# Router products and the norm statistics made as the tiles of the second graph layer finish, and one scale and shift for both norms

## The chip, the cores and the metric

The kernel runs on one NeuronCore of one Trainium2 chip. The metric is the device time of one execution in microseconds. Five engines run side by side and meet only through semaphores: TensorE (PE) for matrix products, VectorE (DVE), ScalarE (ACT), GpSimd (POOL), which here computes the addresses of gathers and scatters, and SyncE (SP), which only starts transfers and relays semaphores.

## The reference

N = 6250 nodes with D = 256 channels, 106250 edges in the first graph layer. Four layers follow each other, each added to its own input:

```python
x = x + gnn0(layernorm(x), ...)          # attention over edges
x = x + slice_ffn(layernorm(x)[None], ...)[0]
x = x + gnn1(layernorm(x), ...)          # attention over the same edges
x = x + experts(layernorm(x)[None], ...)[0]

def experts(x):                          # cut to what matters
    logits = x @ Wr + br                 # Wr is 256 x 8
    top_p, top_idx = top 2 of softmax(logits)
    weights = top_p / top_p.sum(-1)
    xn = (x - mean(x)) * rsqrt(var(x) + 1e-5)       # the second norm
    xe = xn[None] * ln_g[:, None] + ln_b[:, None]
    h = gelu(einsum('end,edh->enh', xe, W1) + b1);  y = einsum('enh,ehd->end', h, W2) + b2
    return (weights * y of the two chosen experts).sum(1)
```

The experts layer is given `layernorm(x)`, so the router sees a normed row, and the experts see a row that has been normed twice.

## The kernel before, in words

The nodes lie on 128 partitions in QT = 49 tiles of 128 rows (`K["x"]`, 128 x 49 x 256 in SBUF, node order sorted by degree). The program runs in stages: `sort_nodes`, `graph` layer 0, `slice_ffn`, `graph` layer 1, `experts`. A stage is a block in which each engine has its own instruction stream, and a barrier ends it.

**`graph` (L713), both layers.** Each tile of nodes has a run of chunks; a chunk holds C = 4 edges for each of the 128 nodes. There are 232 chunks in a layer, about 4.7 for each tile. How many a tile has is a number read at run time, so `by_tile` (L768 and on) is a loop over tiles around a loop over chunks, with the first ("opens") and last ("closes") chunk of a tile written out apart. For each chunk: SP loads the records (L791) and relays to the others that rows have landed (L796); POOL issues four gathers of 128 rows (L826) into a ring of R = 4 chunk buffers, and takes a buffer again only when DVE has made that chunk's messages (`msg_ok`); DVE makes the attention scores (L1017, L1020, L1022, L1023), ACT the exponentials (L915 to L920), DVE rescales the running sums (L987) and makes the messages (L980), and PE sums them in PSUM (L864, L866). When DVE has made the messages of a tile's first chunk it runs `finish` for the tile before (L989 to L999): the denominator, its reciprocal, the division into `fin`, and the addition to `K["x"]`. The next chunk's L1017 stands right behind `finish` on DVE. Layer 0 has another `finish` (without L999), and its DVE does more for each chunk: L967 on 128x1024 and a reduction L1013 over 128x1088 instead of L1017 and L987.

**`experts` (L1552), first block: the router.** On SP: loads of `wr`, `br`, eight of 1 MB of W2 (L1631), small ones, then the stores of the rows `xall` to HBM (`tok`, L1640, seven groups). On POOL: a few iotas, then 49 scatters of `K["x"]` into the output (L1832). DVE makes the statistics of the first norm with BN_STATS in a loop of seven tiles an iteration (`Norm.statistics`, L130 to L135), and their variance (L141 to L147); ACT takes the square root (L1690); DVE the reciprocal and the bias (L152, L153). Then a loop over tiles runs on three engines: ACT norms the tile twice (L1696 into `xrow`, L1697 into `xall`), PE transposes it (L1653), ACT copies the transpose out of PSUM (L1705), PE multiplies it with `wr` (L1662), DVE adds `br` (L1740) and takes the statistics of the normed tile for the second norm (L128). Only then can DVE choose the two best experts of each row (L1751 to L1759), ACT scale and shift `xall` once more (L1721), and DVE and PE build the lists of rows of each expert: ranks from a product with a triangle (L1675), positions (L1774 to L1796), and 98 pairs of one-hot tiles (L1802, L1803) which PE multiplies (L1684). L1818 is DVE's last instruction of the block. The second block runs the experts; PE bounds it.

`Chain.link` (L60) makes an instruction count up a semaphore and the next one wait for it.

## Time and profile before

| | |
|---|---|
| median of 3 runs | 5204.4 us (5200.88 to 5206.28) |
| span of the profiled execution, first to last instruction | 5182.1 us |
| median of the runs less that span | 22.3 us |
| busy: PE / DVE / POOL / ACT | 3347.4 / 2375.1 / 2286.8 / 1277.0 us |

The profile gives no time of the profiled execution other than its span; what lies around the span is taken to be the 22.3 us. Stages by the trace: graph layer 0 from about 504 to 2146 us, slice_ffn to 2609, graph layer 1 to 4176, router block to 4375, experts to the end. "Busy" leaves out register, branch and semaphore instructions; the trace lists those of DVE as "DVEq". "idle before" is the time in which an engine ran nothing before an instruction, with what ended it; "issue" means that the profile shows nothing that it waited for.

### The profile page before, as it was taken

Reading aid. Unit: us, or ns where it says so; the run is one execution under the profiler, and the core shown is the slowest. Engines: PE = TensorE matmul, PEld = TensorE weight load, DVE = VectorE, ACT = ScalarE, POOL = GpSimd, SP = SyncE. Lnnn points to the kernel's source line nnn. Section 1 sums busy time; section 2 is a strip of 40 time slices with the busy share of each in tenths; the row PEclk is TensorE's granted clock in tenths of the full one; section 3 lists DMA queues with packets and bytes.
Section 4 is the critical chain, followed back from the end, with each engine's and each line's share of the span. In section 5 each row is a group of like instructions: output and inputs, shape, how many; then the busy total and the mean of one; then the engine's idle time right before and its main releaser. Section 6 shows DMA issues by size and latency. Waiting matters only on the chain. (4 is left out here: it accounts for less than half of the span.)

```text
span 5182.1 us, 77256 instructions
## 1 busy us (share of the span) xinstructions
PE 3347.4 (65%) x13712; PEld 2377.0 (46%) x13713; DVE 2375.1 (46%) x5239; ACT 1277.0 (25%) x5289; POOL 2286.8 (44%) x2343
## 2 busy tenths in 40 slices
PE   4500676767777777598935545554555537999998
PEld 3300343444444444365823333333333335889887
DVE  4500566656666666776434444444444436111111
ACT  2200333333333333242300000000000034333333
POOL 5160555555555555200355555555555540333333
PEclk9855888888888888798967777777777757999999
DMA  8441333333333333200133333333333342666665
GB/s 200 127 127 32 81 81 76 82 76 81 84 83 81 81 79 83 49 0 1 47 78 86 82 84 85 85 86 84 84 85 85 85 124 96 172 171 171 172 171 136
DMA packets 298776, 489.07 MB, mean 94 GB/s; under 512 B 151906, under 2 KB 199984, under 8 KB 298216
## 3 DMA queue, kind: packets, MB, share of 16 engines
q0 software_dynamic: 127312, 325.41, 25.7%
q1 hardware_dynamic: 158637, 158.21, 10.4%
q10 hardware_dynamic: 12770, 4.81, 0.4%
q8 instruction: 21, 0.34, 0.0%
q14 instruction: 36, 0.29, 0.0%
HBM read 430.09 MB, written 58.63 MB: 94 GB/s over the span
## 5 line engine op out<-in xcount | busy, mean ns | idle before, releaser
L826 POOL DMA_INDIRECT g_rows<-rows,g_recs x1856 | 1759.0, 948 | 1562.6 <-DVE g_msg L980 832.2
L864 PE MATMUL g_pA<-g_msg,k_ident 128*128 128x264 f32 x3712 | 1102.1, 448 | 150.8 <-DVE g_msg L980 91.1
L864 PEld LDWEIGHTS g_pA<-g_msg,k_ident 128*128 128x128 f32 x3712 | 795.0, 225 | 501.3 <-issue 360.7
L855 PE MATMUL g_pE<-g_ew,g_recT 128*128 128x512 f32 x936 | 597.0, 772 | 419.3 <-ACT g_recT L895 373.7
L866 PE MATMUL g_pA<-g_accs,k_ident 128*128 128x264 f32 x928 | 353.6, 467 | 663.4 <-DVE g_accs L987 517.0
L980 DVE TENSOR_TENSOR g_msg<-g_rows,g_pp 128x1024 f32 (+1 forms) x464 | 564.9, 1218 | 417.4 <-ACT g_pp L920 332.3
L915 ACT ACTIVATE g_msg<-g_dd (+1 forms) x464 | 113.5, 245 | 1827.8 <-DVE g_dd L1023 1228.3
L866 PEld LDWEIGHTS g_pA<-g_accs,k_ident 128*128 128x128 f32 x928 | 185.6, 220 | 766.2 <-DVE g_accs L987 570.8
L855 PEld LDWEIGHTS g_pE<-g_ew,g_recT 128*128 128x128 f32 x936 | 202.7, 233 | 648.4 <-issue 584.6
L1969 PE MATMUL e_pY<-e_w,e_hT 128*128 x1632 | 375.1, 383 | 22.6 <-issue 21.9
L1958 PEld LDWEIGHTS e_pH<-e_xT,e_w 128*128 128x128 f32 x3264 | 382.3, 193 | 5.2
L1958 PE MATMUL e_pH<-e_xT,e_w 128*128 128x128 f32 x3264 | 382.7, 276 | 0.0
L1916 POOL DMA_INDIRECT out<-e_ys,e_goal x102 | 160.7, 1576 | 493.8 <-issue 468.7
L1969 PEld LDWEIGHTS e_pY<-e_w,e_hT 128*128 128x128 f32 x1632 | 301.9, 190 | 72.6 <-issue 34.8
L1013 DVE TENSOR_REDUCE g_al<-g_prod (+1 forms) x232 | 296.9, 1280 | 72.0 <-issue 69.6
L967 DVE SCALAR_TENSOR_TENSOR g_prod<-g_pE,g_dall (+2 forms) x232 | 284.2, 1225 | 89.1 <-issue 68.2
L2054 DVE TENSOR_TENSOR e_ys<-e_pY,k_x 128x256 f32<-128x256 f32 x102 | 43.3, 424 | 577.1 <-PE e_pY L1969 577.1
L938 ACT ACTIVATE g_accs<-g_pA,g_cs 128x33 f32 x1464 | 285.9, 305 | 59.9 <-issue 36.2
L2011 ACT ACTIVATE e_hT<-e_pH,e_b 128x128 f32<-128x128 f32 x816 | 222.2, 383 | 44.7 <-issue 42.0
L987 DVE TENSOR_TENSOR g_accs<-g_pA,g_cs 128x264 f32 x232 | 146.6, 632 | 161.3 <-issue 132.1
L1998 ACT ACTIVATE e_xT<-e_pX,e_bl,e_gl 128x128 f32<-128x128 f32 x204 | 82.4, 454 | 470.8 <-PE e_pX L1941 470.8
L1017 DVE TENSOR_TENSOR g_al<-g_rows,k_sdst (+2 forms) x232 | 44.3, 191 | 331.5 <-issue 302.3
(410 smaller groups left out, 3575.4 us busy)
## 6 DMA issues: line engine op xcount, KB each, us to landing
e_w<-in_L_ffn_W SPq DMA_DIRECT2D x110, 1024.0 KB
g_rows<-rows,g_recs POOLq DMA_INDIRECT x1856
g_recs<-slots SPq DMA_DIRECT2D x468, 8.0 KB
tok<-e_xall SPq DMA_DIRECT2D x7, 910.0 KB
rows<-p_row SPq DMA_DIRECT2D x50, 119.0 KB
own<-p_row SPq DMA_DIRECT2D x50, 119.0 KB
p_x<-in_x SPq DMA_DIRECT2D x1, 5600.0 KB
own<-p_x SPq DMA_DIRECT2D x1, 5600.0 KB
```

Source lines behind the costliest of these rows:

```text
L826: pool.indirect_dma_start(out=rows[:, r, j, :], out_offset=None, in_=rows_d, in_offset=bass.IndirectOffsetOnAxis(ap=recs[:, r, 4 * j:4 * j ...
L855: last = t_.matmul(pE[:, b, c:c + 512], recT[:, b, :], ew[:].rearrange("p c d -> p (c d)")[:, c:c + 512], start=True, stop=True)
L864: t_.matmul(pA[:, b, 0:MW], K["ident"][:], msg[:, b, j, :], start=(j == 0), stop=False)
L866: t_.matmul(pA[:, b, 0:MW], K["ident"][:], accs[:], start=False, stop=True).then_inc(agg_ok, 1)
L938: last = s.activation(to[:, h, :], of[:, h, :], ACT.Copy, scale=cs[:, 0, h:h + 1])
L967: v.scalar_tensor_tensor(to, row_of(pE[:, b2, :]).rearrange("p (c h w) -> p c h w", c=C, h=H), 0.0, over(by_head(row_of(dall[:, bass.ds(t, ...
L980: v.tensor_tensor(to, of, by, ALU.mult).then_inc(msg_ok, 1)
L1013: ch.link(v.reduce_sum(sc, prod[:, b2, :, :].rearrange("p a g w -> p (a g) w"), axis=AX), wait=False)
L1916: pool.indirect_dma_start(out=out, out_offset=bass.IndirectOffsetOnAxis(ap=goal_b[b][:, 0:1], axis=0), in_=ys[:, b, :], in_offset=None, bo ...
L1958: last = t_.matmul(pH[b][c][:, j, :], w1[:, b, k, units], xT[:, b, k, :], start=(k == 0), stop=(k == 1))
L1969: last = t_.matmul(pY[b][:], hT[:, b, k, :], w2[:, bass.ds(e, 1), k, :].rearrange("p a h -> p (a h)"), start=(k == 0), stop=(k == KC - 1))
L2011: last = s.activation(hT[:, b, c * HK + j, :], pH[b][c][:, j, :], ACT.Gelu, bias=b1[:, bass.ds(e, 1), c * HK + j])
```

## The change

It acts on graph layer 1 and on the router block.

In graph layer 1, `finish` no longer ends with the addition of the tile to `K["x"]`. Behind it DVE takes BN_STATS of the tile (for the first norm), multiplies the unnormed tile with all eight columns of Wr at once (128 x 8 x 256 products; Wr lies transposed and copied to all partitions) and sums over the 256 channels, into `raw`, 8 numbers for each row. Wr's copy is a transfer of 128 x 2048 floats, 1 MB, at the head of SP's stream, and DVE sums it over channels once (`wsum`) before the first chunk.

The router block has no loop any more. With r = 1/std, the logits are raw * r + nbias * wsum + br. The second norm's variance follows from the first one's: the normed row has mean 0 and variance a * r * r, so `std2` is sqrt(a * r * r + eps), and both norms together are one scale and one shift. ACT norms `xall` straight from `K["x"]`, once: seven tiles before the exponential, 42 behind it.

```diff
@@ graph, layer 1
+            norm, wsum, raw = K["norm"], K["wsum"], K["raw"]
+            wr = m.sb(L + "wr", [Q, X, D])
+            by_expert = m.sb(L + "by_expert", [Q, X, D])
@@ block.sync
                 n2 = groups(sp, K)
+                if not first_layer:
+                    sp.dma_start(wr[:].rearrange("p e k -> p (e k)"), ins["L1_ffn_Wr"]...broadcast_to([Q, X * D])).then_inc(wr_in, 16)
@@ block.vector
                 dve.wait_ge(w_zero, 3)
+                if not first_layer:
+                    dve.wait_ge(wr_in, 16)
+                    v.reduce_sum(wsum[:], wr[:], axis=AX)
@@ finish
-                    fc = Chain(dve, fch, (2 if first_layer else 3) * t)
+                    fc = Chain(dve, fch, (2 if first_layer else 6) * t)
...
-                        v.tensor_tensor(to, to, fin[:], ALU.add).then_inc(x_ok, 1)
+                        fc.link(v.tensor_tensor(to, to, fin[:], ALU.add))
+                        norm.tile(v, t, xk[:, bass.ds(t, 1), :])
+                        fc.link(v.tensor_tensor(by_expert[:], over(to, 1, X), wr[:], ALU.mult))
+                        fc.link(v.reduce_sum(row_of(raw[:, bass.ds(t, 1), :]), by_expert[:], axis=AX), wait=False)
@@ experts, block.sync
-                    sp.dma_start(wr[:], ins["L1_ffn_Wr"]...).then_inc(w_in, 16)
@@ experts, block.tensor: turn, product and their loop go
@@ experts, block.scalar
-                    normed (L1696, L1697), turned (L1705) and their loop
                     act.wait_ge(stats2, 1)
-                    s.activation(norm2.rstd[:], norm2.rstd[:], ACT.Sqrt).then_inc(sq2, 1)
+                    s.activation(std2[:], std2[:], ACT.Sqrt).then_inc(sq2, 1)
+                    act.wait_ge(rst2, 1)
+                    def normed(t):
+                        s.activation(xall[:, t, 0:D], x3[:, t, :], ACT.Identity, bias=norm.nbias[:, t:t + 1],
+                                     scale=norm.rstd[:, t:t + 1]).then_inc(row_ok, 1)
+                    for t in range(GT):
+                        normed(t)
                     act.wait_ge(e_in, 1)
                     s.activation(best[1][:], best[1][:], ACT.Exp).then_inc(e_out, 1)
+                    for t in range(GT, QT):
+                        normed(t)
@@ experts, block.vector
-                    norm1.statistics(dve, v, x3)
...
-                    logits (L1736 to L1740) and its loop, norm2.variance
+                    ch.link(v.tensor_tensor(std2[:], norm.a[:], norm.rstd[:], ALU.mult))
+                    ch.link(v.tensor_tensor(std2[:], std2[:], norm.rstd[:], ALU.mult))
+                    v.tensor_scalar(std2[:], std2[:], LN_EPS, None, ALU.add).then_inc(stats2, 1)
+                    dve.wait_ge(rst1, 1)
+                    v.tensor_tensor(tmp[:], over(norm.nbias[:], 2, X), over(wsum[:], 1, QT), ALU.mult)
+                    ch.link(v.tensor_tensor(lg[:], raw[:], over(norm.rstd[:], 2, X), ALU.mult))
+                    dve.wait_ge(w_in, 16)
+                    v.tensor_tensor(tmp[:], tmp[:], over(br[:], 1, QT), ALU.add)
+                    dve.wait_ge(sq2, 1)
+                    ch.link(v.reciprocal(std2[:], std2[:]))
+                    ch.link(v.tensor_tensor(lg[:], lg[:], tmp[:], ALU.add))
+                    v.tensor_tensor(norm.rstd[:], norm.rstd[:], std2[:], ALU.mult)
+                    v.tensor_tensor(norm.nbias[:], norm.nbias[:], std2[:], ALU.mult).then_inc(rst2, 1)
...
-                    norm2.scales(v, ch, rst2)
```

## Rows read from the trace of the kernel before

**Rows 1.** Busy time by stretch: stretch, length, PE, PEld, DVE, ACT, POOL busy, clock, DMA share, GB/s.

```profile
518.50:2142.00 1623.50, 1154.16 (x3465) 670.75 (x3465) 1010.82 (x1530) 572.33 (x2890) 868.35 (x917) 0.86 0.32 80
2622.00:4170.30 1548.30, 804.10 (x2310) 530.91 (x2310) 660.21 (x1579) 99.64 (x693) 872.58 (x921) 0.74 0.34 84
4175.70:4305.40 129.70, 62.66 (x294) 57.13 (x294) 50.19 (x165) 63.45 (x149) 48.90 (x56) 0.51 0.38 115
4305.40:4375.50 70.10, 46.78 (x204) 32.63 (x204) 65.82 (x258) 25.97 (x52) 0.00 (x0) 0.79 0.27 94
```

**Rows 2.** Waits of POOL, 2622 to 4170 us: waiter, releaser, us in total, times, longest.

```profile
POOL g_rows L826 <- DVE g_msg L980: 388.8, 104, 8.7
```

**Rows 3.** Waits of DVE in the same stretch.

```profile
DVE g_al L1017 <- issue: 302.3, 122, 12.0
```

**Rows 4.** Line L826, 2622 to 4176 us: durations in ns (min/median/max), first and last start.

```profile
L826 POOL DMA_INDIRECT g_rows<-rows,g_recs x921: 941/947/1086, 2621.3 to 4154.4; - x185
```

**Rows 5.** Timeline of DVE around one finish: start, length, what, idle before.

```profile
2889.84 1.22 DVE L980 TENSOR_TENSOR g_msg<-g_rows,g_pp 128x1024 f32 x1 [0.26 <-issue]
2891.14 0.17 DVE L991 TENSOR_SCALAR g_den<-g_pA 128x8 f32 x1
...
2892.26 0.42 DVE L999 TENSOR_TENSOR k_x<-k_x,g_fin 128x256 f32 x1
2892.88 0.19 DVE L1017 TENSOR_TENSOR g_al<-g_rows,k_sdst  x1 [0.20 <-issue]
...
2895.18 1.22 DVE L980 TENSOR_TENSOR g_msg<-g_rows,g_pp 128x1024 f32 x1 [0.24 <-ACT g_pp L920]
```

**Rows 6.** Timeline of POOL over the same finish.

```profile
2891.85 0.95 POOL L826 DMA_INDIRECT g_rows<-rows,g_recs  x1 [4.59 <-DVE g_msg L980]
...
2897.19 0.95 POOL L826 DMA_INDIRECT g_rows<-rows,g_recs  x1 [0.64 <-issue]
```

**Rows 7.** Groups of DVE instructions over the span: count, busy, mean ns of one.

```profile
L1013 DVE TENSOR_REDUCE g_al<-g_prod x231 | 295.7, 1280 | 69.6 <-issue 69.6
L1281 DVE TENSOR_TENSOR f_lg<-f_lg,f_top 128x512 f32<-128x512 f32 x49 | 33.9, 692 | 1.7
L1280 DVE TENSOR_REDUCE f_top<-f_lg 128x8 f32<-128x512 f32 x49 | 33.6, 686 | 1.7
L128 DVE BATCH_NORM_STATS2 e0b_st<-e_xall x48 | 20.5, 427 | 15.8 <-issue 13.7
```

**Rows 8.** Timeline of DVE in the router block.

```profile
4176.86 12.19 DVE L128 BATCH_NORM_STATS2 e0a_st<-k_x  x37 [1.24 <-PEq L106]
...
4212.50 0.10 DVE L1729 MEMSET e0a_na<- 128x49 f32 x1 [2.42 <-issue]
...
4214.69 0.47 DVE L152 RECIPROCAL e0a_rstd<-e0a_rstd 128x49 f32<-128x49 f32 x1 [0.31 <-issue]
...
4305.44 0.56 DVE L1751 TENSOR_REDUCE e_best<-e_lg 128x49 f32<-128x392 f32 x1
4306.03 0.57 DVE L1752 TENSOR_TENSOR e_tmp<-e_lg,e_best 128x392 f32<-128x392 f32 x1
...
4374.18 0.22 DVE L1818 TENSOR_SCALAR e_first_of<-e_second 128x106 f32<-128x106 f32 x1
```

**Rows 9.** Line L133, the statistics loop's branch, 4176 to 4187 us: ns min/median/max.

```profile
L133 DVEq COMPARE_BRANCH  x4: 56/61/69, 4178.3 to 4184.1; - x4
```

**Rows 10.** The same branch, 4190 to 4216 us.

```profile
L133 DVEq COMPARE_BRANCH  x2: 696/1042/1389, 4196.3 to 4214.5; - x2
```

**Rows 11.** Line L1832, POOL's scatters of the router block.

```profile
L1832 POOL DMA_INDIRECT out<-k_x,k_pt x49: 957/963/1556, 4177.9 to 4238.7; - x49
```

**Rows 12.** Timeline of SP in the router block.

```profile
4317.01 20.95 SPq L1640 DMA_DIRECT2D tok<-e_xall  x7
```

**Rows 13.** Timeline at the head of graph layer 1.

```profile
2609.42 2.41 SPq L791 DMA_DIRECT2D g_recs<-slots  x4
...
2612.48 0.99 POOL L826 DMA_INDIRECT g_rows<-rows,g_recs  x1 [13.94 <-DMA g_recs<-slots]
```

**Rows 14.** The chain that ended last: start, length, what.

```profile
4375.50 5.19 DMA k_x<-in_L_ffn_b
```

More of the change, by code:

```diff
@@ L1615, in experts @@
             pL = m2.ps("e0_pL", [Q, 512])
-            pT = [m2.ps(f"e0_pT{b}", [128, 2, 128]) for b in range(2)]
-            pG = [m2.ps(f"e0_pG{b}", [Q, X]) for b in range(2)]
             pR = m2.ps("e0_pR", [Q, 512])
@@ L1627, in _ @@
                 def _(sp):
-                    sp.dma_start(wr[:], ins["L1_ffn_Wr"].rearrange("(k p) e -> p k e", p=128)).then_inc(w_in, 16)
                     sp.dma_start(br[:], ins["L1_ffn_br"].unsqueeze(0).broadcast_to([Q, X])).then_inc(w_in, 16)
@@ L1700, in turned @@
-                    def turned(t, b, early):
-                        act.wait_ge(t_ok, t + 1)
-                        if not early:
-                            act.sem_inc(pace, 1)
-                            act.wait_ge(g_ok, t - 1)
-                        s.activation(xtT[:, b, :, :], pT[b][:, :, 0:Q], ACT.Copy).then_inc(xtT_ok, 1)
-                    def group(u, first, last_group):
-                        for b in range(3 if last_group else 2):
-                            if b < 2 or not last_group:
-                                normed(2 * u + (b + 1), (b + 1) % 2)
-                            turned(2 * u + b, b % 2, first)
@@ L1716, in _ @@
+                    for t in range(GT):
+                        normed(t)
                     act.wait_ge(e_in, 1)
                     s.activation(best[1][:], best[1][:], ACT.Exp).then_inc(e_out, 1)
-                    act.wait_ge(rst2, 1)
-                    for t in range(QT):
-                        s.activation(xall[:, t, 0:D], xall[:, t, 0:D], ACT.Identity, bias=norm2.nbias[:, t:t + 1],
-                                     scale=norm2.rstd[:, t:t + 1]).then_inc(row_ok, 1)
+                    for t in range(GT, QT):
+                        normed(t)
@@ L1727, in _ @@
                     ch = Chain(dve, vch)
-                    norm1.statistics(dve, v, x3)
-                    ch.link(v.memset(norm1.a[:], 0.0))
-                    norm1.variance(v, ch, stats1)
+                    ch.link(v.memset(norm.a[:], 0.0))
+                    norm.variance(v, ch, stats1)
                     dve.wait_ge(sq1, 1)
-                    norm1.scales(v, ch, rst1)
-                    dve.wait_ge(w_in, 32)
-                    def logits(t, b):
-                        dve.wait_ge(xt_ok, t + 1)
-                        norm2.tile(v, t, xt[:, bass.ds(t, 1), :])
-                        dve.wait_ge(g_ok, t + 1)
-                        dve.sem_inc(pace, 1)
-                        v.tensor_tensor(lg[:, bass.ds(t, 1), :].rearrange("p a c -> p (a c)"), pG[b][:], br[:], ALU.add).then_inc(g_used, 1)
-                    with dve.Fori(0, NU) as u:
-                        for b in range(2):
-                            logits(2 * u + b, b)
-                    logits(QT - 1, 0)
-                    ch.link(v.memset(norm2.a[:], 0.0))
-                    norm2.variance(v, ch, stats2)
+                    norm.scales(v, ch, rst1)
+                    ch.link(v.tensor_tensor(std2[:], norm.a[:], norm.rstd[:], ALU.mult))
[11 more added lines that the diff above has]
+                    v.tensor_tensor(norm.nbias[:], norm.nbias[:], std2[:], ALU.mult).then_inc(rst2, 1)
                     dve.wait_ge(iotas, 5)
@@ L2078, in layouts @@
         "L0_ffn_WxT": T(np.asarray(inputs["L0_ffn_W_x"]).T),
+        "L1_ffn_Wr": T(np.asarray(inputs["L1_ffn_Wr"]).T),
     }
@@ L2100, in program @@
         slice_ffn(nc, K, ins, dr)
+        K["norm"] = Norm(m, "k_n", Q, QT, 7)
+        K["wsum"] = m.sb("k_wsum", [Q, X])
+        K["raw"] = m.sb("k_raw", [Q, QT, X])
         graph(nc, K, ins, dr, 1)
```

42 lines of the change are left out of this document (5 added, 37 removed).

## The prediction

> **What bounds the kernel now.** I read the chain that ended last first: it lies in the experts block, PE bound, which the change leaves alone. So the question is what the two stretches ahead of it wait for, and I read busy time by stretch, then waits, then timelines. Graph layer 1 takes 1548.3 us from its first to its last messages, in which POOL is busy 872.58 and DVE 660.21 [rows 1]: neither is full. POOL waits 388.8 us for DVE's messages, in 104 waits [rows 2]. DVE stands 302.3 us ahead of L1017 with nothing in the profile that it waited for [rows 3]. So the loop is a ring: POOL, 1.25 us for each of 4 gathers (0.947 busy [rows 4] and 0.30 between, start to start in [rows 6]: 2897.19 - 2891.85 = 5.34 with a wait of 0.64 where 0.30 is usual), may be four chunks ahead and no more, and DVE, which gives buffers back, halts now and then. POOL's own floor is 232 x 5.0 = 1160 us; 1548 - 1160 = 388 is its waiting, so what DVE's delays add to POOL's waits is what they add to the time. In the router block the loop on ACT, PE and DVE sets the pace: 129.7 us up to the choice of experts, of which DVE is busy 50.19 and PE 62.66 [rows 1]. Behind it the lists keep DVE busy 65.82 of 70.10 us [rows 1]: that part is DVE bound and stays as it is.
>
> **Router block, what goes.** From DVE's first instruction (4176.86) to the first maximum over the logits (4305.44) are 128.6 us [rows 8]. The new path between the same two points: memset, variance, root, up to the reciprocal, as before, 4214.69 - 4212.50 = 2.2 [rows 8]. Then reciprocal (0.47) and bias (0.24, taken as half of a reciprocal): 0.7 with the gap. Three more instructions on 128x49 for std2: 0.7. Then four on 128x392, the two products and the two sums, at 0.60 start to start (4306.03 - 4305.44 = 0.59): 2.4, one reciprocal 0.5, two on 128x49 0.5. Sum 7.0. Gain 128.6 - 7.0 = **121.6 us**. br is now SP's first transfer and has 5 us to land. ACT's first seven norms lie beside DVE's choice of experts. From there to L1818 are 4374.18 - 4305.44 = 68.7 us as now, so the block's DVE ends 76 us behind its start. Two things are late next and stay just behind: POOL's 49 scatters last from 4177.9 to 4238.7 + 1.56 = 4240.3 [rows 11], 63.4 us into the block, and the stores of tok, 20.95 us for seven [rows 12], which can start when SP has passed W2 (8 MB; at the 1 MB in 5.2 us of [rows 14] that is 42 us): 63 us, and some 7 more beside the scatters. Margin 6 us; the cost is 0, bound 0 to 10.
>
> **The stalls.** The statistics loop has 49 instructions. 37 of them take 12.19 us in all, and the remaining 12 take until 4212.50, 23 us [rows 8]. The branch of the same loop takes 0.061 us in the first iterations [rows 9] and 0.696 to 1.389 later [rows 10]. What began in between is POOL's unbroken row of scatters. I take it that register, branch and wait instructions of all engines are slow while POOL works through a long row of them; straight instructions with fixed addresses are not: the memset, the seven instructions of the variance and ACT's root all lie between 4212.50 and 4214.69 [rows 8], in the middle of the slow stretch. The new block has hardly any register instruction, so I charge it nothing; if it kept all stalls (128.6 less 16 for 49 statistics, 61 for 49 turns at 1.25 of four matmuls and norms, and 5 of chains: 46), the gain were 121.6 - 46 = 75.
> The Trainium skill says in "Runtime: NRT & Kernel Launch", Instruction fetch mechanics, that a taken branch whose target has left the two-page window costs a fetch, and prefers unrolled code. By that rule the gain would be the same 121.6, and finish, longer code in a loop, would pay more. The trace speaks against it as the cause here: the same loop ran five iterations free and then slowly [rows 9, 10].
>
> **finish, what comes.** Per tile: statistics 0.43. The products, 2048 elements for each partition: 692 ns for 512, and 1.03 ns an element (from the two reductions, (1280 - 686) / (1088 - 512)) give 0.69 + 1536 x 0.00103 = 2.28. The sum over channels: 1.280 + 960 x 0.00103 = 2.27 [rows 7]. Links 0.2. Together 5.2 us, 49 times, 255 us of DVE work. It stands between L999 and the next chunk's L1017, which follows at once (0.20 idle [rows 5]): its rows have long landed. So the messages of that chunk, 2.30 us behind L1017 [rows 5], come 5.2 us later, and POOL waits for exactly these: it restarted at 2891.85, was through four gathers and waited 0.34 more before 2897.19 [rows 6]. So each tile adds about 5.2 us to POOL's waits at this place. That is the upper end, **255 us**, if nothing is given back.
> What gives back: POOL's waits are now 388.8 / 49 = 7.9 us a tile, most of them at the end of a long row of gathers, in which DVE's register instructions go slow, until POOL runs dry. A break of 5 us in each tile cuts these rows. If no row were long enough any more, POOL would wait only 5.5 a tile: 49 x (5.5 - 7.9) = **-118 us**, the lower end. The other measure is layer 0, the same loop with more DVE work in each chunk: DVE is busy 1010.82 against 660.21, and the loop takes 1623.5 against 1548.3 [rows 1]; 350.6 us of work cost 75.2, 21%. At that rate 255 cost 55. But there the work is spread and here it comes in a lump. By a tile of five chunks: restart of POOL behind the delayed messages, rows of three or four chunks (15 to 20 us), one dry stretch of about 5, the opening chunk's gathers 5, the wait behind finish 5.2, about 34.5 where 5 x 6.67 = 33.4 are spent now; by a tile of four 30.2 against 26.7. With three tiles in four of the first kind: 0.75 x 1.1 + 0.25 x 3.5 = 1.7 a tile, 83 us. I take **90**, nearer to this than to the 55 since the lump always meets a waiting POOL, and keep -118 and 255 as ends.
> GpSimd's side of it: L826 has min, median and max of 941, 947, 1086 ns over 921 gathers [rows 4], though L999 reads two tiles of SBUF for 0.42 us beside them. The products read two for 2.28 us. If they held POOL's gather for their length, the four gathers that run beside finish would end 2.3 later, 7.3 us behind their start, and POOL would still wait for the messages that come 9.8 behind it: no cost in the forecast, but 49 x 2.3 = 112 us where that wait is gone, as in rival B, for whose chance I therefore take 0.23 instead of 0.25. The Trainium skill states such a lock in "SBUF — State Buffer", section "Who interferes with whom": a DVE instruction with two SBUF inputs contends with a GpSimd instruction that reads SBUF. By its rule products and gathers collide; the row shows no trace of it for shorter instructions.
>
> **The rest.** The last tile's finish stands in front of the barrier: 5.2 us in full (in the 255 it counts as one of 49; as the others count at 90 / 48, I add it apart). The 1 MB of Wr goes ahead of the records on SP's queue: such a transfer takes 5.19 us [rows 14], the records now 2612.48 - 2609.42 = 3.1 [rows 13], so the first gather is 2.1 later (bounds 0 and 5.2). The sum of Wr over channels, 2.3 us, lies beside the first gathers. The experts block is unchanged.
>
> **Sum.** -121.6 + 90 + 5.2 + 2.1 = -24.3. Against the profiled execution: 5182.1 becomes 5157.8; with the 22.3 us around it, 5204.4 - 24.3 = **5180 us**. 0.2% (10 us) is what a measurement here can tell from none.
>
> **Rivals.**
> (B) The graph takes the work as layer 0 does, or better: 0 to 55 us. For it: the 21%. Against: the lump. 5204.4 - 121.6 + 7.3 + 30 = 5120.
> (C) The dry stretches stay beside the new waits. Place: POOL's gathers behind each finish. Price: 3 to 5.2 us a tile, 147 to 255 us. It decides from 104 / 49 = 2.1 us a tile on: then the graph loses what the router wins. For it: [rows 6], no slack; and the eight or so register instructions that finish gains. At 4 us a tile: 5204.4 - 121.6 + 7.3 + 196 = 5286, slower.
> (D) The router block gives part back: slow register instructions, or the scatters and stores end last. Gain 75, so 5204.4 - 75 + 97 = 5227. For it: POOL scatters through four fifths of the block. Against: the variance chain.
> (E) The change does what it says, in any case: there is no router loop left to keep.
>
> **Chances.** Forecast 0.37 (0.32 of it faster, 0.05 within 0.2%), B 0.23 (faster), C 0.28 (0.25 slower, 0.03 same), D 0.12 (0.08 slower, 0.02 same, 0.02 faster). Faster 0.57, same 0.10, slower 0.33. The forecast's own range is 5150 to 5200; over the cases, 8 in 10 lie in 5115 to 5270: half of C above it and the far end of B below are left out.
>
> **What would show it.** Right: DVE's first maximum 7 to 9 us behind the block's first DVE instruction; L1818 near 76 us; finish longer by 5.2 us a tile with products and sum at 2.3 each; POOL's waits for messages up from 388.8 to about 480; graph layer 1 about 1640 us. Wrong: POOL's waits below 430 (B) or above 530 (C); router block over 90 us (D); a median of L826 above 0.95 us (gathers held by the products).

## The result, and the profile after

The changed kernel takes 5275.1 us (median of 3 runs, 5272.4 to 5277.2), the one before 5204.4 (5200.9 to 5206.3). The ratio is 1.0141 with a 95% interval of 1.0126 to 1.0155: slower by 1.4%, where 5180 was forecast. The profiled executions took 5275.4 and 5182.1 us of span, 93.3 apart, where the medians are 70.7 apart. Outside the span lie 1.8 us (5277.2 less 5275.4) and not 22.3: the profiled execution before was itself a quick one (the same kernel ran in 5182.7 to 5204.7 us on one chip).

Busy time by stretch, answering to [rows 1], is cut at other points here: first gather of the second graph to start of the last `finish`; to the first maximum over the logits; to the last list instruction; to the end. Columns as there. First the kernel before, in cuts that [rows 1] does not have, then the one after.

```profile
2612.48:4174.31 1561.83, 806.69 (x2320) 532.73 (x2320) 662.67 (x1585) 101.34 (x697) 879.96 (x928) 0.74 0.34 84
4174.31:4305.44 131.13, 62.66 (x294) 57.13 (x294) 51.45 (x169) 63.45 (x149) 48.90 (x56) 0.51 0.38 114
4305.44:4374.40 68.96, 46.78 (x204) 32.63 (x204) 65.78 (x258) 25.97 (x52) 0.00 (x0) 0.80 0.28 95
4374.40:5182.15 807.75, 756.90 (x5100) 700.85 (x5100) 143.21 (x716) 305.85 (x1021) 261.08 (x204) 0.98 0.60 166
```

```profile
2626.12:4349.86 1723.74, 845.06 (x2320) 564.11 (x2320) 893.18 (x1730) 101.76 (x697) 936.23 (x928) 0.70 0.31 76
4349.86:4363.45 13.59, 0.00 (x0) 0.00 (x0) 11.70 (x27) 1.78 (x3) 5.03 (x11) 0.62 0.31 87
4363.45:4467.63 104.18, 51.89 (x204) 36.94 (x204) 67.80 (x256) 25.82 (x51) 44.93 (x45) 0.65 0.64 194
4467.63:5275.40 807.77, 757.39 (x5100) 700.95 (x5100) 143.46 (x717) 306.68 (x1021) 260.89 (x204) 0.98 0.60 166
```

The 93.3 us are: the second graph +161.9, the way to the first maximum -117.5, the list part +35.2, the experts 0, and +13.6 ahead of the graph's first gather. Two of these are losses that were forecast too small: the graph and the list part.

The second graph: the groups of DVE and the waits of POOL, the latter answering to [rows 2]; then its gathers [rows 4].

```profile
L1010 DVE TENSOR_TENSOR g_by_expert<-k_x,g_wr 128x2048 f32<-128x2048 f32 x49 | 111.5, 2275 | 0.0
L1011 DVE TENSOR_REDUCE k_raw<-g_by_expert 128x2048 f32 (+1 forms) x48 | 109.7, 2286 | 6.7
...
L128 DVE BATCH_NORM_STATS2 k_n_st<-k_x (+1 forms) x49 | 20.9, 427 | 11.5 <-issue 5.8
```

```profile
POOL g_rows L832 <- DVE g_msg L989: 516.4, 126, 9.3
```

```profile
L832 POOL DMA_INDIRECT g_rows<-rows,g_recs x928: 942/948/2879, 2626.1 to 4329.9; - x186
```

Product and sum are priced to 0.02 us (2.28 and 2.27 forecast). POOL waits 127.6 us more for messages, and is itself busy 56.3 us more with the same 928 gathers: the median is as before, but the longest is 2.88 us where it was 1.09. One turn of tiles, DVE and then POOL (answering to [rows 5] and [rows 6]):

```profile
3020.79 1.21 DVE L989 TENSOR_TENSOR g_msg<-g_rows,g_pp 128x1024 f32 x1
3022.51 0.17 DVE L1000 TENSOR_SCALAR g_den<-g_pA 128x8 f32 x1 [0.51 <-PE g_pA L872]
...
3024.53 2.27 DVE L1010 TENSOR_TENSOR g_by_expert<-k_x,g_wr 128x2048 f32<-128x2048 f32 x1
3026.94 2.29 DVE L1011 TENSOR_REDUCE k_raw<-g_by_expert 128x2048 f32 x1
```

```profile
3016.72 0.95 POOL L832 DMA_INDIRECT g_rows<-rows,g_recs  x1 [0.30 <-issue]
3022.78 0.95 POOL L832 DMA_INDIRECT g_rows<-rows,g_recs  x1 [5.12 <-DVE g_msg L989]
3025.78 1.84 POOL L832 DMA_INDIRECT g_rows<-rows,g_recs  x1 [2.04 <-issue]
3027.92 0.95 POOL L832 DMA_INDIRECT g_rows<-rows,g_recs  x1 [0.31 <-issue]
3029.18 0.97 POOL L832 DMA_INDIRECT g_rows<-rows,g_recs  x1 [0.30 <-issue]
3033.42 0.94 POOL L832 DMA_INDIRECT g_rows<-rows,g_recs  x1 [3.27 <-DVE g_msg L989]
```

At 3016.72 ends a row of 12 gathers without a break. POOL waits 5.12 us, gets the messages of one chunk, issues four gathers beside `finish`, and waits again, 3.27 us. The long dry stretch (the time in which POOL has no free buffer behind a long row) and the wait behind `finish` stand side by side.

The list part, by its two groups of DVE, and DVE's timeline in it. POOL's 49 scatters run from 4358.4 to 4421.9.

```profile
L1760 DVE TENSOR_SCALAR e_at_hi<-e_iota_q,e_hi,e_code 128x106 f32<-128x106 f32 x98 | 36.8, 376 | 2.5 <-issue 2.3
L1759 DVE TENSOR_SCALAR e_at_lo<-e_iota_q,e_lo 128x128 f32<-128x128 f32 x98 | 32.2, 329 | 30.5 <-issue 19.2 <-PE e_pL L1664 11.3
```

```profile
4387.68 0.29 DVE L1759 TENSOR_SCALAR e_at_lo<-e_iota_q,e_lo 128x128 f32<-128x128 f32 x1 [0.27 <-PE e_pL L1664]
4388.94 0.33 DVE L1760 TENSOR_SCALAR e_at_hi<-e_iota_q,e_hi,e_code 128x106 f32<-128x106 f32 x1 [0.97 <-issue]
4390.50 0.42 DVE L1759 TENSOR_SCALAR e_at_lo<-e_iota_q,e_lo 128x128 f32<-128x128 f32 x1 [1.23 <-issue]
...
4439.64 0.36 DVE L1760 TENSOR_SCALAR e_at_hi<-e_iota_q,e_hi,e_code 128x106 f32<-128x106 f32 x1
4439.89 0.32 DVE L1759 TENSOR_SCALAR e_at_lo<-e_iota_q,e_lo 128x128 f32<-128x128 f32 x1
4440.08 0.36 DVE L1760 TENSOR_SCALAR e_at_hi<-e_iota_q,e_hi,e_code 128x106 f32<-128x106 f32 x1
```

From 4387 on each instruction stands up to 2 us behind the one before it for no reason that the profile names; at 4440, with POOL still, a pair takes 0.44 us.

### The profile page after: what moved, and what is told of

The parts are those of the page before. It is cut to its first block and busy times, and to the rows that moved or that the text cites. A ratio compares the mean times of both kernels' runs of the same rounds, so it can differ in the third digit from the quotient of the medians.

```text
span 5275.4 us, 75930 instructions
## 1 busy us (share of the span) xinstructions
PE 3332.4 (63%) x13418; PEld 2361.9 (45%) x13419; DVE 2568.7 (49%) x5240; ACT 1219.3 (23%) x5142; POOL 2344.3 (44%) x2343
## 5 line engine op out<-in xcount | busy, mean ns | idle before, releaser
L832 POOL DMA_INDIRECT g_rows<-rows,g_recs x1856 | 1815.5, 978 | 1678.3 <-DVE g_msg L989 964.0
L870 PE MATMUL g_pA<-g_msg,k_ident 128*128 128x264 f32 x3712 | 1143.8, 461 | 101.1 <-DVE g_msg L989 67.6
L870 PEld LDWEIGHTS g_pA<-g_msg,k_ident 128*128 128x128 f32 x3712 | 826.6, 234 | 466.2 <-issue 312.4
L872 PE MATMUL g_pA<-g_accs,k_ident 128*128 128x264 f32 x928 | 364.5, 480 | 836.9 <-DVE g_accs L996 702.4
L1926 PEld LDWEIGHTS e_pY<-e_w,e_hT 128*128 128x128 f32 x1632 | 301.9, 190 | 72.7 <-issue 35.2
```

The lines of the kernel that those rows point to most:

```text
L832: pool.indirect_dma_start(out=rows[:, r, j, :], out_offset=None, in_=rows_d, in_offset=bass.IndirectOffsetOnAxis(ap=recs[:, r, 4 * j:4 * j ...
L870: t_.matmul(pA[:, b, 0:MW], K["ident"][:], msg[:, b, j, :], start=(j == 0), stop=False)
L872: t_.matmul(pA[:, b, 0:MW], K["ident"][:], accs[:], start=False, stop=True).then_inc(agg_ok, 1)
L1926: last = t_.matmul(pY[b][:], hT[:, b, k, :], w2[:, bass.ds(e, 1), k, :].rearrange("p a h -> p (a h)"), start=(k == 0), stop=(k == KC - 1))
```

## The experiments

Each group of kernels was timed on one chip together with the kernel before, and the chips turned out to be of two kinds. On A and C, which I call stalling, many register, branch and wait instructions take 0.70 us; on B, D and E, which I call clean, hardly one does. Ratios are to the kernel before on the same chip. A was met twice, the second time with before_gap_paced. Each stretch is from one profiled execution; the times of one kernel on A or C are up to 1% apart, so a stretch there is good to some 15 to 25 us (my estimate).

| chip | kernel | us (median) | ratio, 95% | second graph | to 1st max | lists |
|---|---|---|---|---|---|---|
| A | products_after | 5323.6 | 1.0222 to 1.0280 | 1551.9 | 236.8 | 104.6 |
| A | no_scatter | 5230.0 | 1.0041 to 1.0083 | 1725.8 | 13.6 | 69.0 |
| A | wr_psum | 5274.3 | 1.0128 to 1.0180 | 1720.6 | 13.6 | 104.6 |
| A | late | 5096.1 | 0.9787 to 0.9851 | 1542.5 | 13.6 | 104.2 |
| B | late_psum | 4135.9 | 0.9857 to 0.9889 | 1190.5 | 13.6 | 69.9 |
| B | ring3 | 4233.7 | 1.0090 to 1.0124 | 1288.6 | 13.6 | 69.9 |
| B | late_ring3 | 4207.2 | 1.0026 to 1.0060 | 1264.6 | 13.6 | 69.9 |
| B | late_ring2 | 4452.9 | 1.0617 to 1.0653 | 1505.6 | 13.6 | 69.9 |
| C | after_again | 5189.5 | 1.0091 to 1.0161 | 1669.9 | 13.6 | 103.8 |
| C | before_again | 5122.4 | 0.9975 to 1.0015 | 1534.4 | 131.2 | 69.0 |
| C | late_psum_again | 5085.0 | 0.9900 to 0.9975 | 1553.6 | 13.6 | 103.8 |
| C | split | 5113.1 | 0.9957 to 0.9999 | 1598.9 | 13.6 | 103.8 |
| D | after_third | 4197.7 | 1.0012 to 1.0031 | 1247.4 | 13.6 | 69.9 |
| D | ring3_again | 4238.3 | 1.0101 to 1.0134 | 1290.7 | 13.6 | 69.8 |
| D | late_psum_paced | 4161.3 | 0.9919 to 0.9952 | 1191.4 | 13.6 | 69.4 |
| D | late_psum_gap | 4426.4 | 1.0550 to 1.0585 | 1481.4 | 13.6 | 69.9 |
| A | before_gap_paced | 5041.9 | 0.9812 to 0.9880 | 1477.5 | 106.7 | 69.0 |
| E | late_psum_gap2_paced | 4763.7 | 1.1352 to 1.1383 | 1487.3 | 13.6 | 69.8 |

The kernel before took 5200.8 us on A (5126.3 in the later call), 5119.8 on C, and 4188.2, 4189.0 and 4191.0 on B, D and E.

**products_after.** All products and sums in a row behind the last `finish`.

```diff
-   fc.link(v.tensor_tensor(by_expert[:], over(to, 1, X), wr[:], ALU.mult))
-   fc.link(v.reduce_sum(row_of(raw[:, bass.ds(t, 1), :]), by_expert[:], axis=AX), wait=False)
+   # in end(), behind the last finish
+   for t in range(QT):
+       pc.link(v.tensor_tensor(by_expert[:], over(xk[:, t, :], 1, X), wr[:], ALU.mult))
+       pc.link(v.reduce_sum(raw[:, t, :], by_expert[:], axis=AX))
```

> The 49 products with Wr and the 49 sums stand in a row behind the last finish, with no gather beside them; a finish keeps only its BN_STATS and one wait more than before the change. Theory 1 (the 162 us that second-graph stretch grew by is the DVE lump of product and sum in each finish): the stretch from the first gather to the last finish falls from 1723.7 back to 1562 plus at most 49 x 0.63 = 31, so 1562 to 1593, and the row behind it costs 49 x (2.28 + 2.27 + 0.1) = 228, so the time is 5275 - 146 + 228 = 5357 (5340 to 5375). Theory 2 (something else of the change made the stretch longer: the wait behind the residual sum, BN_STATS, other addresses in SBUF): the stretch stays over 1650 and the time is over 5430. Theory 3 (the products hold the gathers up over a shared SBUF interface): the gathers' mean falls from 1009 ns to 948, and the product alone may be shorter than 2.28 us.

The stretch fell to 1551.9, even 10 under the kernel before, so statistics and the additional wait cost nothing that shows, and product and sum in `finish` cost 1723.7 - 1551.9 = 171.8 us of the 224 that they last. The time was 33 below what was expected, of which the stretch gives some 25. Theory 2 is out. Standing alone, the product takes as long as beside gathers:

```profile
L1058 DVE TENSOR_TENSOR g_by_expert<-k_x,g_wr 128x2048 f32<-128x2048 f32 x49 | 112.3, 2292 | 1.7
```

**no_scatter.** The loop over 49 scatters in the router block is gone, so this kernel's output is incomplete.

```diff
-   for t in range(QT):
-       q = QL if t == QT - 1 else Q
-       pool.indirect_dma_start(out=out, ..., in_=x3[0:q, t, :], in_offset=None).then_inc(x_out, 16)
```

> Leaves out the 49 scatters that put x into out, so the output lacks the residual. Theory 1 (the router's last part, 104.0 us from the first maximum to the last list instruction where before it was 68.7, is stretched by the row of scatters that now runs beside it): that part falls back to 69 (66 to 73), and the time by 31 to 37, to 5241. Rival (the pairs of one-hot and list matmul are slow because their code or the weight loads are, whatever POOL does): part stays at 104 and the time at 5275.

The list part is 69.0 us, to the tenth as before the change (the time fell by more, 45, the span by 37). The same group of DVE as in the changed kernel has lost all of its 30.5 us of idle time:

```profile
L1759 DVE TENSOR_SCALAR e_at_lo<-e_iota_q,e_lo 128x128 f32<-128x128 f32 x98 | 26.4, 270 | 0.0
```

**wr_psum.** The product reads Wr from a copy in PSUM.

```diff
+   wrp = m.ps(L + "wrp", [Q, X, D])
+   v.tensor_copy(wrp[:], wr[:]).then_inc(x_ok, 1)     # once, ahead of the loop
-   fc.link(v.tensor_tensor(by_expert[:], over(to, 1, X), wr[:], ALU.mult))
+   fc.link(v.tensor_tensor(by_expert[:], over(to, 1, X), wrp[:], ALU.mult))
```

> Wr is copied once to PSUM and the product reads it there, so no DVE instruction of the finish's new part reads two SBUF operands. Theory 1 (the lump of DVE time is the cost, whoever reads what): product 2.2 to 2.4 us as before, graph stretch 1723 within 15, time 5275 within 15. Theory 3 (a product with two SBUF inputs holds the gathers, up to 2.88 us for one, 56 us in all on POOL): longest gather under 1.3 us, mean back from 1009 to 948 ns, POOL's busy time in the stretch down 56, and the time down by 30 to 56, to 5219 to 5245.

Half of each theory came: the gathers that theory 3 calls held (they last longer beside the product), and the time that theory 1 expects. The gathers are free again and POOL's busy time fell from 936.2 to 880.5; yet the time is the same, since POOL's waits for messages rose by the same amount, from 516.4 to 569.7.

```profile
L833 POOL DMA_INDIRECT g_rows<-rows,g_recs x928: 943/949/1145, 2624.5 to 4325.5; - x186
```

```profile
POOL g_rows L833 <- DVE g_msg L992: 569.7, 126, 9.4
```

So a product with both inputs in SBUF does hold a gather, about one per tile, and on this chip it holds one that would have waited anyway.

**late.** Statistics, product and sum of tile t-1 stand behind the messages of tile t's last chunk.

```diff
+   def extras(t):
+       ec = Chain(dve, fch, 6 * t + 4)
+       ec.wait()
+       ...                       # BN_STATS, product, sum, taken out of finish
    messages(i)
+   if vscale and closes and not (isinstance(t, int) and t == 0):
+       extras(t - 1)
```

> BN_STATS, product and sum of tile t-1 stand behind the messages of tile t's last chunk instead of in the finish behind the messages of tile t's first chunk; the last tile's stay at the end. Same instructions. Theory 1a (a lump costs because it comes together with the finish, 1.5 us and a wait for PE, at the one point of the tile where POOL's restart hangs on DVE): graph stretch 1620 to 1690, time 5175 to 5240. Theory 1b (a lump costs its share wherever it stands, since every chunk's turn of work passes DVE): stretch 1724 within 15, time 5275 within 15. Theory 3 (the product holds gathers) gives the same mean of about 1.0 us for a gather, and no gain unless the products fall where POOL stands still.

The same work in another place, and the stretch is 181 us shorter, 78 below the lower end of 1a and 19 below the kernel before: the 255 us of DVE work are free there, on this chip. This is a kernel with the router's gain and without the graph's loss, 1.8% faster than the one before (1.5 to 2.1). It still has the longer list part. One turn of tiles in it, DVE and POOL:

```profile
3016.73 1.22 DVE L989 TENSOR_TENSOR g_msg<-g_rows,g_pp 128x1024 f32 x1 [0.26 <-ACT g_pp L926]
3017.87 0.42 DVE L128 BATCH_NORM_STATS2 k_n_st<-k_x  x1
3018.21 2.27 DVE L1015 TENSOR_TENSOR g_by_expert<-k_x,g_wr 128x2048 f32<-128x2048 f32 x1
3020.63 2.29 DVE L1016 TENSOR_REDUCE k_raw<-g_by_expert 128x2048 f32 x1
...
3025.20 1.22 DVE L989 TENSOR_TENSOR g_msg<-g_rows,g_pp 128x1024 f32 x1 [0.26 <-issue]
```

```profile
3015.35 0.94 POOL L832 DMA_INDIRECT g_rows<-rows,g_recs  x1 [5.55 <-DVE g_msg L989]
...
3019.10 2.20 POOL L832 DMA_INDIRECT g_rows<-rows,g_recs  x1 [0.30 <-issue]
...
3027.21 0.95 POOL L832 DMA_INDIRECT g_rows<-rows,g_recs  x1 [0.90 <-DVE g_msg L989]
```

By the whole trace: when the product begins, POOL has on average 5.2 gathers released and not issued, in the changed kernel 2.3. From there to the end of the next messages its breaks of over 0.5 us sum to some 55 us, in the changed kernel to some 185. The held gather (2.20 us) is there too, and costs nothing seen.

**late_psum, late_psum_again.** Late products with Wr in PSUM, on B and then on C.

> The kernel with the late products, and Wr read from PSUM. With Wr in SBUF the late kernel's 47 held gathers cost POOL 68 us of its 1542.5 in the stretch from first gather to last finish. Theory R (what sets the stretch is how long POOL's unbroken rows of gathers get, since DVE, ACT and SyncE stall behind the long ones and POOL then stands idle; a held gather only fills idle time of POOL): gathers back to a mean of 948, stretch 1542 within 20, time 5087 to 5110. Rival P (POOL's work is the bound once the lump is out of the way): stretch down by 40 to 68, time 5025 to 5055.

> Late products with Wr in PSUM. Clean chip: 4136 again. Stalling chip: theory R says that held gathers only fill idle time of POOL there, so stretch 1542 within 20 and time 5087 to 5110; rival P (POOL bound) stretch down by 40 to 68, time 5025 to 5055.

B was a surprise: the kernel before takes 4188 us there, and both graphs are quick for every kernel. On C the stretch was 1553.6, within theory R's 20, and the time 5085 (expected 5087 to 5110). That expectation was built on A's times, and C is quicker: there the kernel before has 1534.4 in this stretch. So the late products are not quite free on C, 19 us over the kernel before where late was 19 under it on A (about as much as one trace can tell), and the kernel is 0.6% faster than before and not 1.8%. Nothing shows that freeing 68 us of POOL brings anything on such a chip; the one comparison within a chip is wr_psum, 3 us.

**ring3, late_ring3, late_ring2.** POOL waits for messages one or two chunks earlier than the ring needs.

```diff
-   pool.wait_ge(msg_ok, 4 * (u - 1) + (r + 1))
+   pool.wait_ge(msg_ok, 4 * (u - 1) + (r + 1 + 1))    # late_ring2: + 2; layer 1 only
```

> The changed kernel, with one edit in the second graph layer: POOL waits for the messages of the chunk three before, not four before, so at most 12 gathers can stand ready and not 16. Products stay in the finish. In the changed kernel 21 rows of 12 gathers and 20 rows of 16 are followed by 5.3 and 7.8 us of idle POOL, 34 rows of 4 by 4.7. Theory R (long rows stall the other engines): rows of 16 go, rows of 8 come, the stretch falls from 1723.7 to 1600 to 1690 and the time to 5150 to 5240. Rival S (a ring with less slack makes POOL wait more often for DVE, and long rows are no cause of anything): the stretch grows by 30 to 120, time 5305 to 5390.

> Late products and the ring of three chunks together. Theory R: rows of 12 and more (20 in the late kernel, followed by 4.8 to 6.2 us of idle POOL) give way to rows of 4 and 8; stretch 1440 to 1520, time 4990 to 5070. Rival S: stretch 1570 to 1660, time 5120 to 5210.

> Late products and a ring of two chunks: at most 8 gathers in a row. Theory R alone would give the least stalls of all, but each chunk's gathers, their landing and DVE's turn (5.0 + 2 + 4 us for two chunks in flight) now bind: stretch 1400 to 1560, time 4950 to 5110. Rival S: every chunk waits for DVE, stretch over 1700, time over 5250.

All three met chip B, on which nothing stalls, so they decide nothing on theory R. They show what slack is worth there: 41 us for ring3 against the changed kernel on D (1288.6 for 1247.4), and 258 for a ring of two (1505.6 against 1190.5 and the 57 that separate the changed kernel from late_psum, see after_third, taken here as the price of Wr in SBUF). A repeat of ring3 met D, clean as well, and gave 1290.7.

> The changed kernel with a ring of three chunks; on the clean chip it took 4234 and says nothing of stalls. Stalling chip, theory R (long rows of gathers stall the other engines): stretch 35 to 125 shorter than the changed kernel's beside it. Rival S (less slack only makes POOL wait more): 30 to 120 longer.

**after_again, before_again, split.** Both kernels unedited on C; split leaves statistics and product in `finish` and puts only the sum late.

> The changed kernel, unedited, because the last four runs came from another chip than the runs before them: there the kernel before took 4188 us, no register or wait instruction took 0.70 us, and POOL's gathers stood in one unbroken row of 487. Call the first kind a stalling chip, the second a clean one. On a stalling chip: 5275 again. On a clean chip POOL's gathers set the graph's time and DVE has slack, so the lump is hidden, the held gathers count in full (+50 to +70), Wr's DMA 3, the router gives 118: 4188 - 118 + 60 + 3 = 4133 (4115 to 4160), faster than before. Rival (the lump costs on a clean chip too): 4188 - 118 + 172 = 4242.

> The kernel before, unedited, for a profile on this chip. Clean chip: graph stretch 945 (928 gathers at 948 ns and the 0.07 us between them, as in the late kernel with Wr in PSUM), list part 69, router 131, and no gather over 1.1 us. Stalling chip: 1562, 69, 131 again.

> BN_STATS and product stay in the finish, only the sum goes behind the messages of the next tile's last chunk. Stalling chip: if what a finish holds costs in proportion (172 us for 5.2 us a tile, 0.67 of it, with nothing for what stands late), 49 x 2.9 x 0.67 = 95 on 1542, so stretch 1637 (1615 to 1660) and time 5190; if there is a threshold at which it begins to cost (2.1 us a tile, by the prediction), 49 x 0.8 = 39, stretch 1581, time 5135; if late work costs as well, 1720. Clean chip: the position makes no difference, 4140 to 4200, as the changed kernel there within 10.

C stalls. There the change costs 135.5 us in the second graph (1669.9 for 1534.4) and 1.3% in all: the first result again. split, against late_psum_again beside it, costs 45 us for 2.9 us in each `finish`, and the changed kernel 116 for 5.2. Steps of 45 and 71 for 142 and 112 us of work: the second part of a lump costs more than the first, 0.32 and 0.63 of what it lasts. The medians rise likewise, by 28 and then 76. Expected were 95 by proportion and 39 by a threshold; the threshold is nearer. It is not a clean pair, since late_psum_again also has Wr in PSUM.

**after_third.** The changed kernel on D.

> The changed kernel on a third or fourth chip. Two of three chips so far stall (before takes 5201 and 5120 us) and one does not (4188). Stalling chip: 1.3 to 1.4% slower than before, as twice already. Clean chip: faster than before by 28 to 73, that is 4115 to 4160, if the lump there hides behind POOL's gathers and only their being held counts; 4242 if the lump costs there too.

D is clean, and the change makes no difference there: 1.0012 to 1.0031. POOL's waits and gathers:

```profile
POOL g_rows L832 <- issue: 253.6, 832, 0.5
POOL g_rows L832 <- DVE g_msg L989: 26.7, 73, 2.1
```

```profile
L832 POOL DMA_INDIRECT g_rows<-rows,g_recs x928: 940/946/3055, 2053.0 to 3287.4; - x186
```

POOL is the bound (928 gathers at 1.25 us are 1160), the lump is hidden (26.7 us of waits), and the held gathers count: 1247.4 against 1190.5 with Wr in PSUM and the late place on B, 57 us, for 67 us more of busy POOL. (The two kernels differ in the place of the products as well, and the chips are two; the waits for messages differ by 8 us.) The expected gain did not come, and part of why is not shown: graph and way to the first maximum together must have taken 4189.0 - 1.8 - 2050 - 69 - 808 = 1260 in the kernel before (2050 is the 2053.1 of this trace less 3 for Wr's transfer), and take 1247.4 + 13.6 = 1261 now. How the 1260 divide was not profiled. If the kernel before took about the 1190 of late_psum in its graph there, its router took about 70 to the first maximum, and not the 131 of a stalling chip: an estimate, by which the router's gain on a clean chip is only some 56 us and the held gathers take it back. The list part lies under the scatters here too (3309.0 to 3373.9, the lists to 3383.9) and takes 69.9, not 104: what slid under the scatters costs on a stalling chip alone.

**late_psum_paced, late_psum_gap.** The scatters in rows of six; and POOL waiting at every second chunk for the chunk before to land.

```diff
    pool.indirect_dma_start(out=out, ...).then_inc(x_out, 16)
+   if t % 6 == 5:
+       pool.wait_ge(x_out, 16 * (t + 1))                                # paced
...
    pool.wait_ge(msg_ok, 4 * (u - 1) + (r + 1))
+   if vscale and r % 2 == 0:                                            # gap
+       pool.wait_ge(rows_in[r - 1], 16 * C * (u + 1) if r else 16 * C * u)
```

> Late products, Wr from PSUM, and the router's 49 scatters in rows of 6, each row waiting for its landing (8 waits of about 2 us). Stalling chip: list part from 104 to 69 to 80, time 24 to 35 below that of late products with Wr in PSUM. Rival (any scatters beside the list, in long rows or short, slow it): list part 95 to 115. Clean chip: list part 70 as before, time unchanged within 5 if the longer scatters (79 us) stay within what the router takes anyway, else up to 10 more.

> Late products, Wr from PSUM, and POOL waits at every second chunk until the gathers of the chunk before have landed, so that no row is longer than 8 gathers (10 us). Stalling chip, theory R: rows of 12 to 19 and their 5 to 8 us of idle POOL go, 116 waits of about 2 us come; stretch 1400 to 1520 where late products with Wr in PSUM have 1554. Rival S: the waits come on top, stretch 1650 to 1780. Clean chip: about 945 + 116 x 1.5 = 1120.

On clean D both are only a cost: 25 us for the paced scatters against late_psum on B (0 to 10 expected; the part behind the lists takes 828.5 for 805.4, so the scatters end last), and 290 us for the gaps (1481.4 for 1191.4), where 1120 was expected, from 945 taken for the base by mistake.

**before_gap_paced.** The kernel before with both pauses, nothing else, and on chip A, which stalls.

> The kernel before, with two pauses for POOL: in the second graph it waits at every second chunk until the chunk before has landed (rows of at most 8 gathers), and in the router after every 6th scatter until they have landed. Stalling chip, theory R (long rows stall the other engines): the pauses cost about 290 us of POOL's time, as late products with Wr in PSUM showed on a clean chip (1191 to 1481), but nearly all of what they cost comes back from stalls: stretch 1480 to 1580 where the kernel before has 1534 to 1562, register and wait instructions of 0.70 us fewer than half of 720, and the router's 131 from last finish to first maximum down to 85 to 110. Rival S (stalls have another cause and the pauses come on top): stretch 1780 to 1850, router 131 or more. Clean chip: stretch 1450 to 1500, and the router 85 to 110, since its 131 was a time with stalls; if that router takes 131 on a clean chip too, the stalls beside the scatters cost it nothing.

Here theory R, that long rows of gathers stall the other engines, is tested, and what it expects comes. Pauses that cost 290 us where nothing stalls leave this kernel 84 us quicker in all (5041.9 for 5126.3, 1.5%), 24 of it in the router (106.7 for 131.1), so some 60 in the second graph. The stretch is 1477.5; it was 1561.8 in the first trace, when the kernel before took 5201 on A, and 1534.4 on C, where it takes 5120, which is the nearer comparison: 57. Of the register, branch and wait instructions that took 0.70 us, there are some 25 where there were some 720 between 2620 and 4150 us. POOL's waits, and the branch of the statistics loop (answering to [rows 9] and [rows 10], here over all of the loop):

```profile
POOL g_rows L829 <- DMA g_rows<-rows,g_recs: 321.5, 113, 4.7
POOL g_rows L829 <- issue: 259.6, 799, 2.6
...
POOL g_rows L829 <- DVE g_msg L983: 4.6, 15, 0.3
```

```profile
L133 DVEq COMPARE_BRANCH  x7: 50/56/69, 4050.8 to 4062.6; - x7
```

The waits for messages, 388.8 us before [rows 2], are 4.6: the pauses (321.5) have taken their place and are shorter in sum. The pauses also bound how many gathers are under way at once, so whether it is the length of POOL's rows or the number of transfers in flight that slows the others is not separated.

**late_psum_gap2_paced.** Everything together, the gaps in both graph layers.

> All that helped together: late products, Wr in PSUM, POOL waiting at every second chunk for the landing of the chunk before (in both graph layers), scatters in rows of 6. Stalling chip, theory R: first layer's gathers 1460 to 1590 where the kernel before has 1585 to 1624 (its rows are shorter already, so least certain), second stretch 1480 to 1530 (the lump hides in POOL's pauses), 14 to the first maximum, list part 69 to 80 instead of 104, then 805 to 825: 4900 to 5040, below the kernel before by 2 to 5%. If lists stay at 104 with scatters in rows of 6, scatters slow them in any row. Clean chip: 4426 + 290 + 20 = 4740 (4680 to 4780), 13% slower than before there.

It met clean E: 4763.7 us, 13.7% slower than the kernel before, as expected for that case (4680 to 4780). What it takes on a stalling chip is open, and so is the list part beside paced scatters there.

## Why the prediction was wrong

**The router's way to the first maximum: right.** 117.5 us gained from last `finish` to first maximum, that holds the last tile's 5.2; forecast were 121.6 - 5.2 = 116.4. This is on the kind of chip that the rows came from. The maximum comes 6.3 us behind the block's first DVE instruction (7.0). That the variance chain passes the scatters unslowed was read rightly from [rows 8].

**"From there to L1818 are 68.7 us as now", and "I charge it nothing": wrong, 35.2 us.** The rows on which it stood showed one engine's instructions with fixed addresses. The list part is a ping-pong of DVE and PE: nearly each of 98 pairs waits for a semaphore on both sides, and waits were in my own list of what goes slow. That the waits are what goes slow here is not shown: the trace lists 2 instructions of DVE's sequencer in this part and none of 0.70 us, and the lost time stands as idle time before ordinary instructions (19.2 us of it "issue", 11.3 behind PE). Before the change the scatters were over (4240.3) when this part began (4305.4); the change moved it under them. I had asked what is late next, and not which work comes to lie beside the scatters. no_scatter shows it whole, and a clean chip, where the same overlap costs nothing (69.9), shows that the overlap alone is not enough. By this the bound of 0 to 10 was too narrow; rival D, with its 46 us, held the size under another name.

**finish, the DVE work: right.** 5.2 us a tile, product and sum within 0.02 us.

**"I take 90": wrong, 162 us.** This is the failed step that decides. It assumed that a break of 5 us in each tile shortens the rows of gathers and so the dry stretches. In the changed kernel rows of 15 gathers and more (a row ends at a break of over 0.5 us) became more frequent, 28 for 17 in the whole graph and 28 for 15 on C, and rows of 4 are followed by 4.7 us of idle POOL, where it was 1.6. The new waits came on top of the old ones: 127.6 us more, and 56.3 more of busy POOL. The sum of the turn had a slip as well: 20 + 5 + 5 + 5.2 is 35.2 and not 34.5, which gives 0.75 x 1.8 + 0.25 x 3.5 = 2.2 a tile, 109 us and not 83, still 53 short. The comparison with layer 0 (21%) fails for the reason that I gave and then weighed too little: there the work is spread over chunks. late shows that it is not the amount but the place that costs: the same work costs 162 us in `finish` in the first trace and, behind the last chunk's messages, nothing on A; on C it is 136 and 19. Rival C was the one that came: "the dry stretches stay beside the new waits", its point at 2.1 us a tile, 162 / 49 = 3.3 measured, 5286 foreseen at 4 us a tile, and 5275 came, though with 35 of it from the lists: that the two times lie so close is luck. It had 0.28.

**The held gathers: seen, and rightly put at nothing on this chip.** The forecast put nothing for them, up to 112 where POOL does not wait. Measured: 56 us more of busy POOL, of which wr_psum brings back 3 in the stretch and 1 in the time, and some 57 on a clean chip, about half of the 112: one gather a tile is held by 1.2 us on average, not by the product's 2.3. The rule of the Trainium skill in "SBUF — State Buffer", section "Who interferes with whom", holds here: 45 gathers over 1.5 us with Wr in SBUF, none with Wr in PSUM. The sign that I named, a median of L826 above 0.95, could not have shown it, since one gather in 20 is held: the maximum and the mean (1009 for 948 ns) do.

**The fetch rule.** The rule of the Trainium skill in "Runtime: NRT & Kernel Launch", Instruction fetch mechanics, I had set aside as the cause of the slow branches. before_gap_paced bears this out: the same loop, the same code, with POOL's rows shortened, has no branch over 69 ns where it had one of 1389.

**The rest.** Wr's transfer cost 5.0 us between the graphs (488.7 for 483.7 from last to first gather) and not 2.1, within its bounds; 8.6 more came from the stages ahead, which the change does not touch. The sum from what was measured: -117.5 + 161.9 + 35.2 + 5.0 + 8.6 = 93.2. The medians grew by 70.7 only; the other 22.6 are the quick execution in which the kernel before was profiled. Against the forecast's -24.3 the graph was 72 too low, the lists 35, the rest 10.

**Left open.** Why moving the lump shortens the long rows as well (10 rows of 15 and more in late, 28 after the change), and so how much of the 181 us is idle POOL at the lump and how much are stalls, is not separated. That POOL has more in hand at the late place is read from late's trace on A and does not carry over: on C late_psum_again has 4.9 gathers in hand and POOL's breaks at the lump still sum to 190 us, and yet the stretch is 116 us shorter than the changed kernel's. The place is shown as the cause; why the late place is cheap is not. Late products and pauses together were not timed on a stalling chip, and a shorter ring not at all there. What makes a chip stall is not known, nor whether it is the chip or a state that it is in; only A was met twice, and it stalled both times.

## What to carry to other kernels

Work that is given to an engine with idle time costs by where it stands in its order, not by how much it is: try it behind the release that lets the other engine run on with most in hand, and measure the alternatives, since here the same 5 us a tile cost 162 us or nothing where the kernel before took 5200, 136 or 19 on another chip, and were hidden on a clean one. When a change takes work away, look at what slides into its place in time, above all at handshakes between engines beside a long row of GpSimd's DMAs: here 35 us on one kind of chip, nothing on the other. A median hides an event that strikes one instruction in twenty.

## What the runs showed of the hardware

- The same program took 22 to 24% longer on some chips than on others: 5120 to 5201 us on two, 4188 to 4191 on three. The experts part, PE bound, takes 803 to 812 us on both kinds (829 and 832 with paced scatters on a clean chip). On the first kind, many register, branch and wait instructions of DVE, ACT and SP take about 0.70 us while GpSimd works through a long row of indirect DMAs; on the second a row of 815 gathers, without a break over 0.4 us, passed without one of them. The same branch in the changed kernel's first trace and on D:

```profile
L775 DVEq COMPARE_BRANCH  x134: 43/56/730, 2641.2 to 4342.2; - x134
```

```profile
L775 DVEq COMPARE_BRANCH  x134: 43/56/80, 2068.0 to 3289.9; - x134
```

- On a stalling chip the other engines' instructions go slow only when POOL's row has lasted some 6 us. Of DVE's register, move and branch instructions in the second graph, 54 of 1776 were slow (0.65 to 0.80 us) in the first 6 us of a row, and 120 of 170 from 12 us on (kernel before; changed kernel: 1 of 1616 and 155 of 218; on D none of 3575 in rows of any age). POOL's idle time behind a row grows with its length: 1.6 us behind 4 gathers, 3.5 behind 8, 5.7 behind 12, 7.5 behind 16 (kernel before). Making GpSimd wait can therefore make a kernel faster there, by 1.5% in before_gap_paced; on a clean chip such pauses left kernels 5.7% (late_psum_gap) and 13.7% (late_psum_gap2_paced) slower than the kernel before.
- A DVE product of 2.27 us with both inputs in SBUF holds a gather by up to 2.1 us; with one input in PSUM it lasts 2.27 us as well and holds none.
